# DLRM tower, one core: first two one-hot fields looked up as a couple, tile 3's rows at other places, one ScalarE copy for two lookups

## The chip, the cores and the metric

One core of one Trainium2 chip. The metric is the device time of one execution in microseconds (us); lower is better. Engines are named as in the profile: PE (TensorE matmul), PEld (its weight load), DVE (VectorE), ACT (ScalarE), POOL (GpSimd), SP (SyncE, here a DMA queue).

## What is computed

The reference, cut to what matters:

```
e  = stack([tbl_f[ids[:, f]] for f in range(26)], axis=1)   # 512 x 26 x 128, float32
T  = concatenate([r_dense[:, None, :], e], axis=1)          # 512 x 27 x 128
Z  = einsum('bnd,bmd->bnm', T, T)[:, iu0, iu1]              # 351 dot products a sample
h  = concatenate([Z, r_dense], axis=1)                      # 512 x 479
h  = maximum(h @ W_top1 + b_top1, 0)                        # 512 x 512
h  = maximum(h @ W_top2 + b_top2, 0)                        # 512 x 256
y  = h @ W_top3                                             # 512 x 1
```

Twelve of the 26 tables are large (12500 or 125000 rows) and 14 are small (1000 or 1250 rows).

## The kernel before, in words

**Small tables.** Their 14 fields (places 1 to 14 of XT) are looked up on PE. A table is cut into chunks of 128 rows: 8 chunks for the first six fields, 10 for the last eight, 128 chunks in all. A chunk's one-hot matrix `hot` (128 rows by 512 samples) is made by comparing the broadcast ids `ids_bc` with a row number, and PE multiplies the chunk with it, once for the high part `t_hi` (L473) and once for the low part `t_lo` (L475), adding up in one of six PSUM banks. ACT makes `t_hi` (L594) and DVE `t_lo` (L708). `t_hi` and `t_lo` have three places each, `table` five, `hot` eight chunks.

Fields 2 to 13 are looked up in couples: the table of an even number holds the first half of both fields' chunks, field by field in turn, the odd one the second half, so that one instruction makes the one-hots of two chunks (128x1024). Fields 0 and 1 are single (`SINGLES = 2`), each one-hot 128x512. Most one-hots are made by DVE (L739). ACT makes some in two steps: `distance` (L612, |ids - row|, into `apart`) and `one_hot` (L623, relu(1 - distance)). For the single fields that is every fifth one-hot, for tables 3 and 5 to 13 (`ACT_TABLES`) the last one of the table; table 4 has none.

A finished lookup bank is copied by ACT into XT (L636, 128x512, destination 32 floats apart), field i-2 in ACT's part of table i. PE waits for such copies only at tables 6, 8, 10 and 12, where a couple's two banks are used again. Field 12 goes by DVE (L744, L745), and field 13 by ACT (L633, L634), in two parts.

**Large tables.** POOL gathers rows by 48 indirect DMAs (L403), a tile of 128 samples and a group of four fields after the other. A step `rows (t, g)` is four PE transposes into `tp` (L457) and one copy from there into XT (L582), by ACT but for the steps in `VECTOR_ROWS`, which are DVE's: before, that is (3, 1).

**The tower.** For each of four tiles there are two halves. `burst` and `gram` are each 32 small matmuls (L431) of a half into one of two PSUM halves; ACT and DVE then drain the half, each two copies to `table` (L566) and eight to `Zt` (L574). A half's bank is used again two halves later, and `burst` waits for that drain. Some rows of Zt are moved by small DMAs (L328, L364) before layer 1 may read them. `dense` (L415, 8 matmuls) starts layer 1's sum of a tile and `layer1` (L421, 24 matmuls) ends it; DVE's relu (L773) makes h1; `layer2` is L532 and L542.

**Order.** Each engine goes through the list `timeline()` in its order: the 14 one-hot steps with the nine row steps of tiles 0 to 2 among them, then the tower's steps. PE, ACT and DVE each do their own part of a step, one after the other, and wait for semaphores. SP issues the table and id loads in the order of the tables; before, ids of table 4 wait until table 1 has been used up by PE (L337), and everything behind them in the queue waits with them.

The places of low parts in DVE's order:

```
LOW_PARTS = {(i, 5 if i < SINGLES else 4 if OH_CHUNKS[i] == 8 else 6): (i + 1, 0, OH_CHUNKS[i + 1])
             for i in range(1, K_OH - 1)}
LOW_PARTS.update({(0, 0): (0, 0, HEAD), (0, 4): (0, HEAD, OH_CHUNKS[0]), (0, 5): (1, 0, HEAD),
                  (1, 1): (1, HEAD, OH_CHUNKS[1])})
```

Of the kernel before, what the change touches and what calls it, by code (L numbers as in the profile page):

```python
# [29 lines left out]
TILES = BATCH // P  # L30
# [17 lines left out]
VECTOR_ROWS = [(3, 1)]  # L48
IDS = 6
HEADED = 2  # L50
HEAD = 3
PARTS = 3
HOTS = 8
SINGLES = 2
# [4 lines left out]
ACT_EVERY = 5  # L59
ACT_TABLES = [3, 5, 6, 7, 8, 9, 10, 11, 12, 13]  # L60
# [37 lines left out]
LOW_PARTS = {(i, 5 if i < SINGLES else 4 if OH_CHUNKS[i] == 8 else 6): (i + 1, 0, OH_CHUNKS[i + 1])  # L98
             for i in range(1, K_OH - 1)}
LOW_PARTS.update({(0, 0): (0, 0, HEAD), (0, 4): (0, HEAD, OH_CHUNKS[0]), (0, 5): (1, 0, HEAD),  # L100
                  (1, 1): (1, HEAD, OH_CHUNKS[1])})


def timeline():

    steps = []
    for i in range(K_OH):
        steps.append(("onehot", 0, i))  # L110
        steps += [("rows", t, g) for t, g in ROWS_AFTER.get(i, [])]
    steps += [("dense", 0, 0), ("burst", 0, 0), ("gram", 0, 0), ("burst", 0, 1), ("gram", 0, 1), ("rows", 3, 0),
              ("burst", 1, 0), ("gram", 1, 0), ("rows", 3, 1), ("burst", 1, 1), ("gram", 1, 1), ("burst", 2, 0),
              ("gram", 2, 0), ("layer1", 0, 0), ("layer1", 0, 1), ("burst", 2, 1), ("gram", 2, 1), ("dense", 1, 0),
# [3 lines left out]
    return steps  # L118
# [55 lines left out]
def pair_of(i):  # L174

    return i if i < SINGLES else i - (i - SINGLES) % 2


def field_of(i, c):

    return i if i < SINGLES else pair_of(i) + c % 2


def row_chunk(i, c):

# [19 lines left out]
HOT_FIRST = [k for k, i in enumerate(TABLE_OF) if i < SINGLES or (k - first_hot(i)) % 2 == 0]  # L205


def hot_width(m):

    return 1 if TABLE_OF[HOT_FIRST[m]] < SINGLES else 2  # L210


def by_scalar(m):

    i = TABLE_OF[HOT_FIRST[m]]
    if i < SINGLES:
        return m % ACT_EVERY == ACT_EVERY - 1
# [8 lines left out]
def dlrm_tower(nc, dense, ids, ids_oh, tbls, small, w1, w2, tail, ends, out):  # L226
    f32, f32r, i32 = mybir.dt.float32, mybir.dt.float32r, mybir.dt.int32
    ALU, ACT = mybir.AluOpType, mybir.ActivationFunctionType
    with ExitStack() as ctx:
# [67 lines left out]

        def lookup_bank(i):

            return work[:, (i - K_OH + GRAM_BANKS) % LOOKUP_BANKS, :]  # L300
# [31 lines left out]
        def _(sp):  # L332
            def table_ids(i):

                n = 1 if i < SINGLES else 2
                if i >= SINGLES + 2:
                    sp.wait_ge(hot_used, groups_used(first_hot(ids_free(i))))  # L337
                sp.dma_start(ids_bc[:, ids_slot(i):ids_slot(i) + n, :],
                             ids_oh[i:i + n, :, :].rearrange("f p b -> p f b")).then_inc(ids_in[i], 16)
# [246 lines left out]
        def _(act):  # L586
# [15 lines left out]
            def distance(j):  # L602
# [4 lines left out]
                act.wait_ge(ids_in[f], 16)  # L607
                act.wait_ge(rownum_ready, 2)
# [20 lines left out]
            def copy_lookups(f):  # L629
# [5 lines left out]
                else:  # L635
                    nc.scalar.copy(XT[:, :, 1 + f], lookup_bank(f)).then_inc(lookup_copied, 1)  # L636
# [5 lines left out]
            one_hot(mine_in(0)[0])  # L642
            high_part(1, 0, HEAD)
            distance(1)
            high_part(1, HEAD, OH_CHUNKS[1])
            for kind, t, i in STEPS:
                if kind == "onehot":
                    rest = mine_in(i)[1:]
                    if rest and i < HEADED:
                        one_hot(rest[0])  # L650
                    if i + 1 < SINGLES:
                        one_hot(mine_in(i + 1)[0])
                    if i + 2 < K_OH:
# [41 lines left out]
        def _(dve):  # L695
# [28 lines left out]

            low_part(*LOW_PARTS[0, 0])
            for kind, t, i in STEPS:
                if kind == "onehot":
                    f = field_of(i, 0)
                    dve.wait_ge(ids_in[f], 16)
                    n = 1 if i < SINGLES else 2  # L730
                    for c in range(0, OH_CHUNKS[i], n):
# [3 lines left out]
                        if not by_scalar(HOT_FIRST.index(k)):  # L735
                            if k >= HOTS:
                                dve.wait_ge(hot_used, groups_used(k + n - HOTS))
                            v, at = KINDS.index(OH_CHUNKS[i]), row_chunk(i, c)
                            nc.vector.tensor_scalar(hot[:, k % HOTS:k % HOTS + n, :], ids_bc[:, ids_slot(f):ids_slot(f) + n, :],  # L739
                                                    rownum[:, v, at:at + 1], None,  # L740
                                                    ALU.is_equal).then_inc(hot_dve, 1)
# [106 lines left out]
```

## Time and profile before

| what | value |
|---|---|
| times of 3 runs | 118.52, 118.72 and 598.5 us (median 118.72) |
| the profiled execution | 118.53 us, of which the span of the instructions is 116.7 us |
| granted clock of PE | 1.00 over the span |
| busy share of the span | PE 93%, PEld 78%, DVE 73%, ACT 69%, POOL 56% |
| DMA | 17.75 MB, mean 152 GB/s |

The one run of 598.5 us stands alone beside two that agree within 0.2 us. The profiled execution is 1.83 us longer than its span, which is what lies before the first and behind the last instruction. Busy shares are means over stages with different limits.

### The profile page before, as it was taken

Reading aid. Unit: us, or ns where it says so; the run is one execution under the profiler, and the core shown is the slowest. Engines: PE = TensorE matmul, PEld = TensorE weight load, DVE = VectorE, ACT = ScalarE, POOL = GpSimd, SP = SyncE. Lnnn points to the kernel's source line nnn. Section 1 sums busy time; section 2 is a strip of 40 time slices with the busy share of each in tenths; the row PEclk is TensorE's granted clock in tenths of the full one; section 3 lists DMA queues with packets and bytes.
Section 4 is the critical chain, followed back from the end, with each engine's and each line's share of the span. In section 5 each row is a group of like instructions: output and inputs, shape, how many; then the busy total and the mean of one; then the engine's idle time right before and its main releaser. Section 6 shows DMA issues by size and latency. Waiting matters only on the chain.

```text
span 116.7 us, 2626 instructions
## 1 busy us (share of the span) xinstructions
PE 108.4 (93%) x1008; PEld 91.0 (78%) x1008; DVE 85.6 (73%) x179; ACT 80.9 (69%) x151; POOL 65.3 (56%) x66
## 2 busy tenths in 40 slices
PE   4889799899999999999999999989699998998993
PEld 4757478588688887887888788978599987898990
DVE  5699999889597789969778751499996841567131
ACT  4469990994999999999997794499993602455011
POOL 7387787788777877877787775003063720004000
PEclk9999999999999999999999999999999999999999
DMA  3799749999999529992111112001011110001000
GB/s 74 262 361 406 275 105 411 382 398 363 400 316 380 218 71 367 405 338 65 45 45 32 35 45 60 13 0 26 6 23 51 34 32 6 0 3 21 6 3 1
DMA packets 7751, 17.75 MB, mean 152 GB/s; under 512 B 2078, under 2 KB 3002, under 8 KB 7610
## 3 DMA queue, kind: packets, MB, share of 16 engines
q1 hardware_dynamic: 5770, 14.13, 33.1%
q0 software_dynamic: 1824, 3.25, 9.7%
q10 hardware_dynamic: 144, 0.20, 0.6%
q8 instruction: 8, 0.13, 0.5%
q14 instruction: 5, 0.04, 0.1%
HBM read 17.33 MB, written 0.00 MB: 148 GB/s over the span
## 4 chain that ended last, share of the span: by engine, by line
PE 66%; ACT 11%; DMA 8%; DVE 8%; issue 4%; SPq 1%; ACTq 0%; DVEq 0%
PE work L473 20%; PE work L475 19%; DMA table<-small 8%; PE work L431 8%; PE work L421 6%; PE work L532 5%; ACT Zt L574 4%; PE tp L457 4%; DVE hot L739 3%; PE work L415 3%; ACT t_hi L594 2%; ACT table L566 2%; DVE Zt L574 2%; ACT hot L623 2%; DVE t_lo L708 2%
## 5 line engine op out<-in xcount | busy, mean ns | idle before, releaser
L403 POOL DMA_INDIRECT rows<-tbl,idx x48 | 58.4, 1217 | 18.3 <-issue 13.3
L473 PE MATMUL work<-hot,t_hi 128*128 128x512 f32 x128 | 51.8, 405 | 2.2 <-DVE hot L739 1.1
L475 PE MATMUL work<-hot,t_lo 128*128 128x512 f32 x128 | 50.2, 392 | 0.0
L739 DVE TENSOR_SCALAR hot<-ids_bc,rownum 128x1024 fp32r<-128x1024 int32 (+1 forms) x59 | 38.9, 699 | 7.2 <-PE work L475 7.1
L473 PEld LDWEIGHTS work<-hot,t_hi 128*128 128x128 f32 x128 | 24.0, 188 | 10.8 <-DVE hot L739 2.9
L475 PEld LDWEIGHTS work<-hot,t_lo 128*128 128x128 f32 x128 | 24.1, 188 | 4.4
L594 ACT CAST t_hi<-table 128x1280 fp32r<-128x1280 f32 (+3 forms) x16 | 16.8, 1050 | 5.8 <-DMA table<-small 5.5
L708 DVE TENSOR_TENSOR t_lo<-table,t_hi 128x1280 fp32r<-128x1280 f32 (+3 forms) x16 | 19.5, 1217 | 1.2 <-ACT t_hi L594 1.0
L431 PE MATMUL work<-XT 128*58 128x52 f32 x512 | 15.1, 217 | 2.4 <-ACT Zt L574 1.1
L431 PEld LDWEIGHTS work<-XT 128*58 128x58 f32 x512 | 14.3, 133 | 3.7 <-issue 2.4
L328 POOL DMA_DIRECT2D Zt<-table x9 | 4.7, 531 | 22.1 <-DVE table L566 22.1
L612 ACT ACTIVATE apart<-ids_bc,minus_row 128x1024 f32<-128x1024 int32 (+1 forms) x13 | 13.6, 1046 | 0.9 <-DMA ids_bc<-ids_oh 0.9
L574 DVE COPY Zt<-work 17x48 f32<-17x48 f32 (+1 forms) x64 | 12.8, 200 | 1.0
L623 ACT ACTIVATE hot<-apart 128x1024 fp32r<-128x1024 f32 (+1 forms) x13 | 12.5, 962 | 1.5 <-PE work L475 1.4
L636 ACT COPY XT<-work 128x512 f32<-128x512 f32 x12 | 13.3, 1104 | 0.0
L574 ACT COPY Zt<-work 17x48 f32<-17x48 f32 (+1 forms) x64 | 12.6, 196 | 0.8
L582 ACT COPY XT<-tp 128x512 f32<-128x512 f32 x11 | 8.2, 743 | 6.1 <-PE tp L457 5.9
L566 ACT COPY table<-work 14x224 f32<-14x224 f32 x16 | 5.7, 359 | 8.9 <-PE work L431 8.7
L566 DVE COPY table<-work 14x224 f32<-14x224 f32 x16 | 6.1, 380 | 6.2 <-PE work L431 5.9
L421 PE MATMUL work<-Zt,w_sb 128*128 128x128 f32 x84 | 10.2, 277 | 0.0
L421 PEld LDWEIGHTS work<-Zt,w_sb 128*128 128x128 f32 x84 | 9.8, 192 | 0.2
L457 PE MATMUL tp<-ident,rows 128*128 128x128 f32 x48 | 7.3, 274 | 0.0
(47 smaller groups left out, 58.1 us busy)
## 6 DMA issues: line engine op xcount, KB each, us to landing
table<-small SPq DMA_DIRECT2D x8, 640.0 KB, 7.9
ids_bc<-ids_oh SPq DMA_DIRECT2D x6, 512.0 KB, 6.1
table<-small SPq DMA_DIRECT2D x4, 512.0 KB, 7.6
w_sb<-w SPq DMA_DIRECT2D x1, 1024.0 KB, 7.7
rows<-tbl,idx POOLq DMA_INDIRECT x48, 4.1
table<-small SPq DMA_DIRECT2D x2, 320.0 KB, 5.0
ids_bc<-ids_oh SPq DMA_DIRECT2D x2, 256.0 KB, 4.5
w_sb<-w SPq DMA_DIRECT2D x1, 512.0 KB, 8.8
```

Of the source, the lines that this page charges most:

```text
L403: nc.gpsimd.indirect_dma_start(rows[:, t, place - FIRST, :], None, tbls[f], bass.IndirectOffsetOnAxis(ap=idx[:, t, place - FIRST:place - F ...
L421: last = nc.tensor.matmul(l1_block(t, u), w1_sb[:, c, u * P:(u + 1) * P], Zt[:, t, c, :], start=False, stop=c == CHUNKS - 1 and (t == TILE ...
L431: last = nc.tensor.matmul(gr[PAD * s:PAD * s + COUPLED, half, q, 0:COUPLE * FIELDS], XT[:, b:b + COUPLE, :].rearrange("d s n -> d (s n)")[ ...
L473: nc.tensor.matmul(bank, t_hi[:, i % PARTS, c * D:(c + 1) * D], hot[:, k % HOTS, :], start=row_chunk(i, c) == 0, stop=False)
L475: last = nc.tensor.matmul(bank, t_lo[:, i % PARTS, c * D:(c + 1) * D], hot[:, k % HOTS, :], start=False, stop=row_chunk(i, c) == n - 1)
L566: return copy(Zlow[:, t % 2, :, first:end:COUPLE], gr[PAD * s:PAD * s + LOW, half, :, column(s):column(s) + LOW].rearrange("n q m -> n m q"))
L574: last = copy(Zt[PAD * g:PAD * g + n, t, :, first:end:COUPLE], gr[PAD * s:PAD * s + n, half, :, column(s) + n - CHUNKS:column(s) + n].rear ...
L594: nc.scalar.copy(t_hi[:, i % PARTS, c0 * D:c1 * D], table[:, i % TABLES, c0 * D:c1 * D]).then_inc(hi_ready, 1)
L612: nc.scalar.activation(apart[:, j % 2, 0:n * BATCH].rearrange("p (f b) -> p f b", f=n), ids_bc[:, ids_slot(f):ids_slot(f) + n, :], ACT.Abs ...
L623: nc.scalar.activation(hot[:, k % HOTS:k % HOTS + n, :], apart[:, j % 2, 0:n * BATCH].rearrange("p (f b) -> p f b", f=n), ACT.Relu, bias=1 ...
L708: nc.vector.tensor_tensor(t_lo[:, i % PARTS, c0 * D:c1 * D], table[:, i % TABLES, c0 * D:c1 * D], t_hi[:, i % PARTS, c0 * D:c1 * D].bitcas ...
L739: nc.vector.tensor_scalar(hot[:, k % HOTS:k % HOTS + n, :], ids_bc[:, ids_slot(f):ids_slot(f) + n, :], rownum[:, v, at:at + 1], None, ALU. ...
```

## The change

- Fields 0 and 1 become a couple like the others (`SINGLES` is gone; all tables are interleaved). Only their first two chunks keep single one-hots (`LONE = 2`), and their ids come by two DMAs of their own at the head of SP's queue. ACT's head part of table 0 is 4 chunks and not 3; table 1 is loaded and split as a whole (`HEADED = 1`), before in two parts. The id places are counted so that the ids of table 4 wait for nothing.
- ACT makes the last one-hot of tables 0, 1, 3, 4, ... 13: table 4 is new, and tables 0 and 1 have one wide one-hot each in place of three single ones in all.
- ACT copies the two lookups of a couple by one instruction of 128x1024, in its part of the next couple's first table; fields 12 and 13 stay as they are.
- `rows (3, 0)` goes in front of the first `burst` and is copied by DVE; `rows (3, 1)` goes behind `layer1 (0, 1)` and is copied by ACT. `dense (0)` goes from in front of the first `burst` to behind `gram (0, 1)`, and `dense (2)` from behind `gram (3, 0)` to in front of `burst (3, 0)`.
- DVE's relu of tile 2 goes into the drain of the last half, in front of its last four copies.

```diff
-VECTOR_ROWS = [(3, 1)]
+VECTOR_ROWS = [(3, 0)]
-HEADED = 2
-HEAD = 3
+HEADED = 1
+HEAD = 4
-SINGLES = 2
+LONE = 2
-ACT_EVERY = 5
-ACT_TABLES = [3, 5, 6, 7, 8, 9, 10, 11, 12, 13]
+ACT_TABLES = [0, 1, 3, 4, 5, 6, 7, 8, 9, 10, 11, 12, 13]
...
+LOW_PARTS = {(i, 4 if OH_CHUNKS[i] == 8 else 6): (i + 1, 0, OH_CHUNKS[i + 1]) for i in range(K_OH - 1)}
+LOW_PARTS.update({(0, 0): (0, 0, HEAD), (0, HEAD): (0, HEAD, OH_CHUNKS[0]), (0, 6): (1, 0, OH_CHUNKS[1])})
...
-    steps += [("dense", 0, 0), ("burst", 0, 0), ("gram", 0, 0), ("burst", 0, 1), ("gram", 0, 1), ("rows", 3, 0),
-              ("burst", 1, 0), ("gram", 1, 0), ("rows", 3, 1), ("burst", 1, 1), ("gram", 1, 1), ("burst", 2, 0),
-              ("gram", 2, 0), ("layer1", 0, 0), ("layer1", 0, 1), ("burst", 2, 1), ("gram", 2, 1), ("dense", 1, 0),
-              ("layer2", 0, 0), ("layer1", 1, 0), ("layer1", 1, 1), ("rows", 3, 2), ("burst", 3, 0), ("gram", 3, 0),
-              ("dense", 2, 0), ("layer2", 1, 0), ("burst", 3, 1), ("gram", 3, 1), ("layer1", 2, 0), ("layer1", 2, 1),
+    steps += [("rows", 3, 0), ("burst", 0, 0), ("gram", 0, 0), ("burst", 0, 1), ("gram", 0, 1), ("dense", 0, 0),
+              ("burst", 1, 0), ("gram", 1, 0), ("burst", 1, 1), ("gram", 1, 1), ("burst", 2, 0), ("gram", 2, 0),
+              ("layer1", 0, 0), ("layer1", 0, 1), ("rows", 3, 1), ("burst", 2, 1), ("gram", 2, 1), ("dense", 1, 0),
+              ("layer2", 0, 0), ("layer1", 1, 0), ("layer1", 1, 1), ("rows", 3, 2), ("dense", 2, 0), ("burst", 3, 0),
+              ("gram", 3, 0), ("layer2", 1, 0), ("burst", 3, 1), ("gram", 3, 1), ("layer1", 2, 0), ("layer1", 2, 1),
...
-                if i >= SINGLES + 2:
-                    sp.wait_ge(hot_used, groups_used(first_hot(ids_free(i))))
...
+                if i >= IDS:
+                    sp.wait_ge(hot_used, groups_used(first_hot(i - IDS + 2)))
...
-            table_ids(0)
+            for f in range(LONE):
+                sp.dma_start(ids_bc[:, f, :], ids_oh[f, :, :]).then_inc(ids_in[f], 16)
...
-                    nc.scalar.copy(XT[:, :, 1 + f], lookup_bank(f)).then_inc(lookup_copied, 1)
+                    nc.scalar.copy(XT[:, :, 1 + f:3 + f],
+                                   work[:, bank_of(f):bank_of(f) + 2, :].rearrange("p f b -> p b f")).then_inc(lookup_copied, 2)
...
             high_part(0, HEAD, OH_CHUNKS[0])
-            one_hot(mine_in(0)[0])
-            high_part(1, 0, HEAD)
-            distance(1)
-            high_part(1, HEAD, OH_CHUNKS[1])
+            high_part(1, 0, OH_CHUNKS[1])
             for kind, t, i in STEPS:
                 if kind == "onehot":
...
+                    if 1 < i < K_OH - 2:
                         high_part(i + 2, 0, OH_CHUNKS[i + 2])
...
+                    for m in mine_in(i):
+                        one_hot(m)
+                        if i == 0:
+                            distance(1)
+                    if i <= 1:
+                        high_part(i + 2, 0, OH_CHUNKS[i + 2])
+                    if i > 1 and pair_of(i) == i:
                         copy_lookups(i - 2)
...
                     copy_high(nc.vector.tensor_copy, t, i, halves % HALVES, first)
+                    if t == TILES - 1 and i == 1:
+                        units_done(t - 1)
                     if t < TILES - 1 or i == 1:
                         copy_high(nc.vector.tensor_copy, t, i, halves % HALVES, second).then_inc(gram_dve, 1)
```

## Rows read from the trace of the kernel before

**Rows 1.** The page's busy times of the engines over the span.

```profile
PE 108.4 (93%) x1008; PEld 91.0 (78%) x1008; DVE 85.6 (73%) x179; ACT 80.9 (69%) x151; POOL 65.3 (56%) x66
```

**Rows 2.** PE's waits, 0 to 75 us: us in total, times, longest.

```profile
PE work L473 <- DVE hot L739: 1.1, 2, 0.7
PE work L473 <- ACT t_hi L594: 0.5, 1, 0.5
PE work L473 <- ACT hot L623: 0.4, 1, 0.4
```

**Rows 3.** The chain that ended last, at table 4: start, us, what.

```profile
24.11 0.23 PE work L475
```

**Rows 4.** Timeline, start-up: start, us, engine, line, what [idle before <-releaser].

```profile
7.50 0.49 ACT L594 CAST t_hi<-table 128x384 fp32r<-128x384 f32 x1
8.58 0.73 ACT L612 ACTIVATE apart<-ids_bc,minus_row 128x512 f32<-128x512 int32 x1 [0.58 <-DMA ids_bc<-ids_oh]
13.72 0.49 PE L473 MATMUL work<-hot,t_hi 128*128 128x512 f32 x1 [0.70 <-DVE hot L739]
```

**Rows 5.** Timeline, 15 to 31 us, tables 2 to 5.

```profile
15.83 0.47 SPq L350 DMA_DIRECT2D table<-small  x1
...
20.63 1.05 ACT L594 CAST t_hi<-table 128x1024 fp32r<-128x1024 f32 x1 [3.10 <-DMA table<-small]
...
22.68 0.50 PE L473 MATMUL work<-hot,t_hi 128*128 128x512 f32 x1 [0.42 <-ACT hot L623]
...
23.97 1.27 ACT L594 CAST t_hi<-table 128x1280 fp32r<-128x1280 f32 x1 [0.29 <-PE work L475]
...
27.99 0.74 ACT L582 COPY XT<-tp 128x512 f32<-128x512 f32 x1 [1.72 <-PE tp L457]
...
30.86 0.50 PE L473 MATMUL work<-hot,t_hi 128*128 128x512 f32 x1
```

**Rows 6.** Timeline, 72 to 84 us, the first halves of the tower.

```profile
72.76 0.94 DVE L745 COPY XT<-work 128x384 f32<-128x384 f32 x1
...
80.21 0.72 ACT L582 COPY XT<-tp 128x512 f32<-128x512 f32 x1
80.42 0.78 DVE L566 COPY table<-work 14x224 f32<-14x224 f32 x2
...
83.49 1.92 PE L431 MATMUL work<-XT 128*58 128x52 f32 x64 [1.09 <-ACT Zt L574]
```

**Rows 7.** The chain that ended last, 95 to 110 us.

```profile
95.62 0.45 PE tp L457 x4
...
96.86 1.92 PE work L431 x64
98.77 1.09 PE work L415 x8
...
106.79 0.70 DVE apart L773
...
107.54 1.99 PE work L532 x8
```

**Rows 8.** Groups by line and shape: xcount | busy us, mean ns | idle before.

```profile
L739 DVE TENSOR_SCALAR hot<-ids_bc,rownum 128x1024 fp32r<-128x1024 int32 x46 | 33.2, 757 | 7.2 <-PE work L475 7.1
L636 ACT COPY XT<-work 128x512 f32<-128x512 f32 x12 | 13.3, 1104 | 0.0
L612 ACT ACTIVATE apart<-ids_bc,minus_row 128x1024 f32<-128x1024 int32 x10 | 11.4, 1143 | 0.0
L623 ACT ACTIVATE hot<-apart 128x1024 fp32r<-128x1024 f32 x10 | 10.6, 1064 | 1.5 <-PE work L475 1.4
L594 ACT CAST t_hi<-table 128x1280 fp32r<-128x1280 f32 x8 | 10.2, 1271 | 0.3 <-PE work L475 0.3
L708 DVE TENSOR_TENSOR t_lo<-table,t_hi 128x1024 fp32r<-128x1024 f32 x4 | 4.9, 1216 | 0.0
```

**Rows 9.** Timeline of POOL: the last gather of `rows (3, 0)`.

```profile
65.77 1.02 POOL L403 DMA_INDIRECT rows<-tbl,idx  x1 [0.31 <-issue]
```

More of the change, by code:

```diff
@@ L296, in dlrm_tower, with bank_of @@
         turn_full, rows_ready, last_ready = sem("turn_full"), sem("rows_ready"), sem("last_ready")
+        def bank_of(i):
+            return (i - K_OH + GRAM_BANKS) % LOOKUP_BANKS
         def lookup_bank(i):
-            return work[:, (i - K_OH + GRAM_BANKS) % LOOKUP_BANKS, :]
+            return work[:, bank_of(i), :]
         def l1_block(t, u):
@@ L729, in _ @@
                     dve.wait_ge(ids_in[f], 16)
-                    n = 1 if i < SINGLES else 2
-                    for c in range(0, OH_CHUNKS[i], n):
+                    for c in range(OH_CHUNKS[i]):
                         if (i, c) in LOW_PARTS and i + c:
@@ L734, in _ @@
                         k = first_hot(i) + c
[L735 to L741, printed above, removed]
+                        if k not in HOT_FIRST or by_scalar(HOT_FIRST.index(k)):
+                            continue
+                        n = hot_width(HOT_FIRST.index(k))
+                        if k == 1:
+                            dve.wait_ge(ids_in[1], 16)
+                        if k >= HOTS:
+                            dve.wait_ge(hot_used, groups_used(k + n - HOTS))
+                        v, at, slot = KINDS.index(OH_CHUNKS[i]), row_chunk(i, c), ids_slot(f) + c % 2
+                        nc.vector.tensor_scalar(hot[:, k % HOTS:k % HOTS + n, :], ids_bc[:, slot:slot + n, :],
+                                                rownum[:, v, at:at + 1], None, ALU.is_equal).then_inc(hot_dve, 1)
                     if i == K_OH - 1:
@@ L768, in _ @@
                 elif kind == "layer1" and i == (1 if t < TILES - 1 else 0):
-                    if t >= 2:
+                    if t < TILES - 2:
+                        units_done(t)
+                    elif t == TILES - 1:
                         dve.wait_ge(l2_full, t - 1)
-                    if t < TILES - 1:
-                        dve.wait_ge(l1_part, 2 * (t + 1))
-                        nc.vector.tensor_scalar(h1[:, t % 2, :, :], l1[:], 0.0, None, ALU.max).then_inc(h1_ready, 1)
-                    else:
                         for u in range(0, BLOCKS, 2):
@@ L833 @@
     for i, n in enumerate(OH_CHUNKS):
-        if i < SINGLES:
-            table = chunks[i]
-        else:
-            f = pair_of(i)
-            part = slice((i - f) * n // 2, (i - f + 1) * n // 2)
-            table = np.stack([chunks[f][:, part], chunks[f + 1][:, part]], axis=2)
+        f = pair_of(i)
+        part = slice((i - f) * n // 2, (i - f + 1) * n // 2)
+        table = np.stack([chunks[f][:, part], chunks[f + 1][:, part]], axis=2)
         arrays[f"small_{i}"] = table.reshape(OH_ROWS, n * D)
```

46 lines of the change are left out of this document (16 added, 30 removed).

## The prediction, made before the changed kernel was run

> **What bounds the kernel now.** I read the page first: PE is busy 93% of the span [rows 1]. So the time is PE's work plus PE's waits, and the next views are PE's waits and the chain that ended last. Up to 75 us PE waits little: twice for a one-hot of DVE, once for a high part, once for a one-hot of ACT [rows 2]. In between it runs one matmul each 0.23 us [rows 3]: a chunk of two is 0.457 us, a table of 8 chunks 3.66 us, one of 10 chunks 4.58 us, and four transposes 0.45 us [rows 7]. That is a floor which the change doesn't touch. Only the waits can go, and they are told by the timeline of the start [rows 4], of tables 2 to 5 [rows 5], of the first halves of the tower [rows 6], and the chain near the end [rows 7]. Prices of single instructions come from the groups by shape [rows 8]. I sum against the profiled execution, 118.53 us (span 116.7 and 1.83 around it); it is 0.2 below the median of the runs shown, 118.72, which I count as no difference. What a measurement of this kernel can tell from no change is put at 2%, 2.4 us.
>
> **Part 1, start-up to the start of table 4.** Before, table 4 starts at 23.71: the matmul at 22.68 is the first of chunk 30, and two chunks lie between, 2 x 0.457 and 0.11 for the restart [rows 5]. Two waits lie ahead of it: PE stands from about 12.9 to 13.72 for chunk 13 [rows 4], and before 22.68 for ACT's one-hot, which came late because ACT had waited 3.10 us for table 5; that load was issued at 15.83 only, behind the ids of table 4, which waited for table 1 to be used up [rows 5].
> The second wait goes: ids of table 4 wait for nothing now, and table 5 is behind the low part of table 0, some 7 us earlier. Worth 0.57 and 0.11 us of restart, 0.68.
> The first is replaced by others. DVE has less to do up to the end of table 1's one-hots: 2 single ones at 0.4 and 5 wide ones at 0.67 (4.15) in place of 13 single ones (5.2), the starts in sequence being some 0.08 closer than the durations; a gain of 1.1. But ACT's chain becomes the late one. Its high part of table 1 needs the whole 512 KB of it. In the queue these end after 24 + 256 + 256 + 256 + 256 + 512 = 1560 KB (ids of the gathers, head of table 0, ids of fields 0 and 1, rest of table 0, table 1). Before, ids of field 1 ended the same 1560 KB and released ACT at 8.55 [rows 4]; the head of table 1 could be cast at 7.50 already [rows 4]. From 8.55: high part of table 1 0.95, one-hot of table 0 0.96, distance 1.04, high part of table 2 0.95 (durations of rows 8 less about 0.1 for the overlap, the 128x1024 cast taken from 1.05 in [rows 5]), that is 12.45; low part of table 2 on DVE, 1.14, then one-hot k = 12, 0.7: 14.35. PE takes chunk 12 then and ends table 1 at 14.4 + 4 x 0.457 = 16.25. Before it ended at 15.3 (13.72 + 0.11 + 3 x 0.457). So 1.0 us is lost here.
> Tables 2 and 3 then run without a wait in my count: DVE comes to k = 28 at 20.6 and has it at 21.3 while PE wants it at 21.8, and ACT has k = 30 at 22.1 against 22.7. Table 4 starts at 16.25 + 2 x 3.66 + some restart = 23.65. Sum of part 1: 1.0 lost, 0.7 and the small gaps of tables 2 and 3 won, -0.06. Bounds: it moves one to one with the landing of table 1. The earliest is 7.6 (after the 984 KB that had landed by 7.50), then -0.95, where DVE's chain also stops it; the latest I take 0.7 behind 8.55, +0.65, since ids of table 4 and table 5 now press behind it and six gathers run beside it.
>
> **Part 2, the wide copy and table 4's one-hot on ACT.** Before, ACT in table 4 is free early and stands 1.72 us before the row copy at 27.99 [rows 5], and still PE gets the last one-hot of table 5 only at 30.86, when it wanted it at 30.59: it follows the row copy and the high part of table 7 in ACT's order. The stall is 0.27 and 0.10 of restart. After: high part of table 6 from T4+0.26 (23.97 for T4 = 23.71) to T4+1.43, one-hot 0.96, distance 1.04, wide copy C less 0.1, so the row copy begins at T4+3.33+C, if that is later than T4+4.28, where the transposes end. From there 0.59, 1.15 and 1.07 to the one-hot of table 5. C is not in the trace. The nearest rows: casts with whole runs of 1280 and 384 elements take 1.27 and 0.49 us [rows 4, 5], 0.87 ns an element and 0.155 fixed. The lone copy, one element in each 128 bytes, takes 1.104 [rows 8], 1.85 ns an element; the row copy, runs of four, takes 0.74 [rows 5], 4.6 ns a run. A break thus costs some 1 ns: for runs of two, 512 x (2 x 0.87 + 1.0) + 0.155 = 1.55 us. Ends: 1.1 (breaks hidden entirely) and 2.2 (two lone copies, nothing won). I take 1.55, the row of runs of four being the nearest. Then the one-hot is there at T4+7.69 in place of T4+7.15: +0.55 us (0.15 at C = 1.1, 1.2 at C = 2.2).
> All later tables have room: an even table's ACT work is 1.17 + 0.96 + 1.04 + C + 0.6, 5.2 us at C = 1.55 against PE's 5.03, but its one-hot is taken before the copy, the next table's is wanted 3.8 us after that table starts, and an odd table's work is only 3.8. DVE gives up table 4's one-hot (0.67), which is hidden under PE and counts nothing. A copy saves ACT 0.6 us a couple, which also counts nothing while PE is the bound.
> On the wide copy the Trainium skill has a rule of its own, in "SBUF — State Buffer", section "Door 1: The DMA port swizzle (why `[64,N]` ≈ `[32,N]`)": SBUF has 16-byte lines, and an access that goes to a new line pays. By it places 1 and 2 lie in one line, but 3 and 4 in two. The rows of lone and four-element runs agree with it as well as with a price of a break. Its result is rival 2.
>
> **Part 3, the tower.** The first burst waited behind `dense (0)` and the lookup copies, and starts at 73.31. Now transposes of `rows (3, 0)` are in its place, 0.45 for 1.05, and the copies' first parts end at 72.94: start 73.0, -0.3. The gather must have landed by 72.3; its last DMA was issued at 65.77 [rows 9] and gathers take 4.1 us on the page, so 69.9. DVE's copy of it lies behind its lookup copy, which ends at 73.7 [rows 6], ends at 74.4, and the first drain begins at 75.0: free. `dense (0)` fills PE's wait for the first drain, 76.75 to 77.7: free.
> Before, ACT's copy of (3, 0) at 80.21 held up the drain, and the third tile's first burst stood 1.09 us, to 83.49 [rows 6]. Without it DVE's drain is late next: DVE's third half begins at 80.42 and takes 2.54, to 82.96. With the 0.3 earlier, burst (2, 0) starts at 82.7: -0.8 in all.
> `rows (3, 1)` was in a wait of PE and now stands in full work, before `burst (2, 1)`: +0.45. Its ACT copy meets an idle ACT.
> `dense (2)`, 1.09, goes into the wait for the copy of (3, 2). Before, from 95.62: 0.45 + 0.79 of wait + 1.92 + 1.09 = 4.24 [rows 7]. After: h1 of tile 1 is ready about 0.77 after the start (0.69 of relu and two hand-overs), then 1.09 + 1.92 = 3.78: -0.45.
> The relu of tile 2: it ended at 107.49 and layer 2 started at 107.54 [rows 7], while `dense (3)` had ended at 107.2. Now the relu is four copies (0.85) earlier, though not before layer 1's end: it ends 0.3 before dense (3) does. -0.34. The four copies behind it end 0.85 later than the relu, 1.4 before layer 1 of the last tile wants them, and the small DMAs for it are as early as all else. Sum of part 3: -0.8 + 0.45 - 0.45 - 0.34 = -1.14. Bounds: -1.5 (if rows (3, 1) hides) and -0.5 (if a small DMA of tile 0 or 3 is late, since burst (2, 0) is sooner and the DMAs' landing isn't).
>
> **Sum.** -0.06 + 0.55 - 1.14 = -0.65: 118.53 - 0.65 = 117.9 us.
>
> **Rivals.**
> 1. Start-up really gains. Table 1 lands at 7.6 to 7.9 as its own pieces did before, DVE's 1.1 us come through, and part 1 is -0.7 to -0.95: 117.0 to 117.2; with C near 1.1 as well, 116.7. For: DVE was what PE waited for twice [rows 2], and the wait at 22.68 goes for certain. Against: ACT's order puts two wide ACT steps ahead of the high part of table 2.
> 2. The copy pays for each line of 16 bytes. As a mechanism of this kernel: a lone element costs 1.85 ns, so a couple that lies in one line costs 1.1 us, one in two lines 0.155 + 512 x 2 x 1.85 ns = 2.05. The copy of fields 2 and 3 (places 3 and 4), the one in table 4, is of the second kind: part 2 is +1.05 in place of 0.55, 118.4 us. This is what the Trainium skill's rule would make of it. For: a lone element and three together give 1.85 + 3 x 0.87 = 4.5 ns, and the row copy shows 4.6. Against: a plain price of a break gives the same.
> 3. The other side: ACT becomes the bound. The wide copy reads two PSUM banks in turn, element by element, which no row shows. If each switch costs as much again as a break and C reaches 3 us, the stall of table 5 is +2.05 and an even and an odd table's ACT work is 6.7 + 3.8 = 10.5 us against PE's 10.06: +0.4 for each of three later couples. 118.53 - 0.06 + 2.05 + 1.3 - 1.14 = 120.7. It decides the sign from C = 2.2 on. Against: the row copy also reads 512 bytes apart and is cheap.
> 4. Start-up loses more: the first wide one-hots need ids of both fields, and table 1 lands at 9.2: +0.65, 118.6.
> That the change doesn't do what it says would be C = 2.2 with nothing saved; it is the end of part 2.
>
> **How the numbers follow.** Forecast (117.4 to 118.3) 0.42, rival 1 0.22, rival 2 0.16, rival 4 0.13, rival 3 0.05, the rest 0.02 for something unseen. The range leaves out rival 3 and the far ends of 1 and 4: 116.5 to 119.3. Faster by over 2% means below 116.3, which needs rival 1 at its end and part 3 at its bound: 0.11. Slower by over 2% is above 121.1, rival 3 and worse: 0.03. Within: 0.86.
>
> **What would show it.** Part 1: table 1's high part starts near 8.5, a PE wait before chunk 12, and table 4 starting near 23.65 with no wait of ACT for table 5. Part 2: a group of six copies 128x1024 with a mean near 1.55 (rival 2: three of 1.1 and three of 2.05), and a PE wait of some 0.8 in table 5 for ACT's one-hot. Part 3: the first burst near 73.5, burst (2, 0) released by DVE 9.7 us after the first, no wait longer than 0.1 before layer 2 of tile 2. The prediction is wrong if the high part of table 1 starts a microsecond from 8.5, if C is beyond 2.2, or if layer 1 of tile 0 waits for its small DMAs.

## The result, and the profile after

The changed kernel took 119.59 us (median of 12 runs, 119.25 to 120.68), the kernel before beside it 119.36; the ratio is 1.0058, with a 95% interval of 1.0031 to 1.0084. A second set of runs gave 1.0052 (1.0017 to 1.0087). So it is 0.5% slower: no change by the bound of 2%, but on the other side of where the forecast put it, and above the range. The profiled execution took 119.52 us, span 117.7, against 118.53 and 116.7. Here and below a median is of all the runs of a set, while a ratio compares only the executions in the usual one of two states that a kernel shows.

The median of the kernel before moved between 118.7 and 119.7 us from one set of runs to the next, more than most single terms here. The verdicts on terms below therefore rest on the marks of the profiles, and on the ratios only for the whole. Most marks repeat to 0.05 us; the landing of table 1 (8.04 to 9.04 us) and the stretch of tables 6 to 13 (39.5 to 41.0) don't.

The page, and PE's waits up to 75 us and behind (us in total, times, longest; they answer to [rows 1, 2]):

```profile
PE 108.7 (92%) x1008; PEld 91.6 (78%) x1008; DVE 83.5 (71%) x171; ACT 79.6 (68%) x144; POOL 62.7 (53%) x66
```

```profile
PE work L467 <- DVE hot L739: 1.4, 2, 1.3
PE work L467 <- ACT hot L619: 1.1, 1, 1.1
PE work L467 <- issue: 0.8, 1, 0.8
PE work L425 <- DVE XT L743: 0.4, 1, 0.4
...
PE work L425 <- DVE Zt L568: 1.2, 2, 0.6
PE work L409 <- DVE apart L720: 0.3, 1, 0.3
PE work L526 <- DVE apart L720: 0.3, 1, 0.3
```

DVE and ACT have less to do than before and PE waits longer for them: one wait of 1.1 us for a one-hot of ACT is new. The timeline of that place (start, us, engine, line), which answers to [rows 5]:

```profile
24.18 1.27 ACT L588 CAST t_hi<-table 128x1280 fp32r<-128x1280 f32 x1 [0.67 <-PE work L469]
25.36 1.05 ACT L619 ACTIVATE hot<-apart 128x1024 fp32r<-128x1024 f32 x1
26.32 1.14 ACT L608 ACTIVATE apart<-ids_bc,minus_row 128x1024 f32<-128x1024 int32 x1
27.36 1.99 ACT L632 COPY XT<-work 128x1024 f32<-128x1024 f32 x1
29.12 0.79 ACT L576 COPY XT<-tp 128x512 f32<-128x512 f32 x1
29.77 1.28 ACT L588 CAST t_hi<-table 128x1280 fp32r<-128x1280 f32 x1
30.93 1.08 ACT L619 ACTIVATE hot<-apart 128x1024 fp32r<-128x1024 f32 x1
...
32.05 0.50 PE L467 MATMUL work<-hot,t_hi 128*128 128x512 f32 x1 [1.10 <-ACT hot L619]
```

Read it from below: PE gets the last one-hot of table 5 at 32.05. ACT had begun it at 30.93, behind a high part, behind the row copy, which began at 29.12 although its transposes had ended at about 28.2; ahead of that stand the new one-hot of table 4, the distance for the one-hot of table 5, and a wide copy of 1.99 us.

The start-up (answers to [rows 4]):

```profile
8.66 1.05 ACT L588 CAST t_hi<-table 128x1024 fp32r<-128x1024 f32 x1 [0.67 <-DMA table<-small]
9.61 1.06 ACT L619 ACTIVATE hot<-apart 128x1024 fp32r<-128x1024 f32 x1
10.57 1.14 ACT L608 ACTIVATE apart<-ids_bc,minus_row 128x1024 f32<-128x1024 int32 x1
11.62 1.03 ACT L588 CAST t_hi<-table 128x1024 fp32r<-128x1024 f32 x1
...
12.69 1.23 DVE L698 TENSOR_TENSOR t_lo<-table,t_hi 128x1024 fp32r<-128x1024 f32 x1 [0.38 <-ACT t_hi L588]
...
14.63 0.50 PE L467 MATMUL work<-hot,t_hi 128*128 128x512 f32 x1 [0.77 <-issue]
```

This is the forecast chain, step by step: high part of table 1 as its DMA lands, one-hot, distance, high part of table 2, low part, one-hot k = 12 (of chunks 12 and 13), PE. The wait for table 5 of [rows 5] is gone.

The tower (answers to [rows 6, 7]), from the timeline:

```profile
74.57 3.62 PE L425 MATMUL work<-XT 128*58 128x52 f32 x128 [0.38 <-DVE XT L743]
...
81.73 1.92 PE L425 MATMUL work<-XT 128*58 128x52 f32 x64 [0.61 <-DVE Zt L568]
...
84.28 1.92 PE L425 MATMUL work<-XT 128*58 128x52 f32 x64 [0.62 <-DVE Zt L568]
...
88.90 0.60 PE L451 MATMUL tp<-ident,rows 128*128 128x128 f32 x4
...
97.62 1.16 PE L409 MATMUL work<-dense_t,w_sb 128*128 128x128 f32 x8 [0.35 <-DVE apart L720]
...
107.75 0.69 DVE L720 TENSOR_SCALAR apart<-work 128x512 f32<-128x512 f32 x1 [0.89 <-PE work L415]
...
108.50 1.99 PE L526 MATMUL work<-w_sb,apart 128*128 128x256 f32 x8 [0.33 <-DVE apart L720]
```

DVE's drain is late next, as forecast, with two waits of 0.6. `dense (2)` fills the wait for the copy of (3, 2). But the relu of tile 2 starts at 107.75 though its matmuls were issued by 107.0, and layer 2 still waits 0.33 us for it.

All profiles cut at the same marks, in us. `T1` is the start of ACT's high part of table 1 in the new start-up; `4` and `6` are PE's starts of tables 4 and 6; `E` is the last lookup matmul; `h0` to `h7` are the starts of the eight halves on PE:

```
kernel             T1     4      4>6   6>E    E>h0  h0>h4  h4>h5  h5>h6  h6>h7  h7>end
before             -      23.71  8.53  39.84  1.22  10.18  4.72   8.64   4.66   15.20
changed            8.66   23.93  9.51  39.93  1.20   9.71  5.16   9.28   3.77   15.19
changed, again     8.80   24.07  9.52  39.97  1.19   9.70  5.20   9.28   3.77   15.19
e1 lone copies     8.78   24.05  8.77  39.54  1.18   9.77  5.16   9.28   3.77   15.20
e2 table 4 DVE     9.04   24.31  8.58  40.96  1.19   9.69  5.16   9.36   3.77   14.85
e3 shifted XT      8.44   23.74  8.56  39.68  1.19   9.72  5.16   9.28   3.77   15.19
e4 tower alone     -      24.07  8.79  39.81  1.94   9.70  5.16   9.28   3.77   14.82
e5 waits           8.04   23.30  9.51  40.12  1.09   9.70  5.20   9.30   3.77   14.75
e6 high 2 first    8.55   23.39  9.49  39.91  1.22   9.70  5.20   9.33   3.77   15.19
e7 all three       8.78   23.62  8.56  40.25  1.08   9.70  5.16   9.28   3.77   14.75
e8 e7, rows (3,1)  8.53   23.37  8.56  39.58  1.07   9.69  4.73   9.28   3.77   14.75
e9 before, shifted -      24.43  8.45  39.62  1.22  10.03  4.92   8.52   4.66   15.18
e10 e7, lone       8.61   23.48  8.70  39.87  1.08   9.70  5.16   9.28   3.77   14.75
e11 start-up alone 8.13   23.40  8.57  39.53  1.22  10.19  4.72   8.64   4.66   15.22
```

Changed less before, first profiles: start +0.22, tables 4 and 5 +0.98, tables 6 to 13 +0.09, tower -0.31 (-0.02 - 0.47 + 0.44 + 0.64 - 0.89 - 0.01). That makes +0.98, beside +1.0 of the span and +0.99 of the profiled executions. The start's +0.22 is smaller than what the landing of table 1 alone moves it from run to run.

### The profile page after: what moved, and what is told of

Same layout as the page of the kernel before. It is cut to its first block, busy times and chain, and to the rows that moved or that the text cites. A ratio compares the mean times of both kernels' runs of the same rounds, so it can differ in the third digit from the quotient of the medians.

```text
span 117.7 us, 2615 instructions
## 1 busy us (share of the span) xinstructions
PE 108.7 (92%) x1008; PEld 91.6 (78%) x1008; DVE 83.5 (71%) x171; ACT 79.6 (68%) x144; POOL 62.7 (53%) x66
## 4 chain that ended last, share of the span: by engine, by line
PE 74%; DVE 9%; ACT 6%; DMA 4%; issue 4%; SPq 1%; ACTq 0%; DVEq 0%
PE work L467 23%; PE work L469 21%; PE work L415 8%; PE work L425 8%; PE work L526 5%; DMA table<-small 4%; DVE Zt L568 4%; PE tp L451 3%; DVE table L560 2%; PE work L409 2%; ACT hot L619 2%; PE work L536 2%; ACT t_hi L588 2%; DVE apart L720 1%; PE tp L415 1%
## 5 line engine op out<-in xcount | busy, mean ns | idle before, releaser
L397 POOL DMA_INDIRECT rows<-tbl,idx x48 | 55.8, 1163 | 20.3 <-issue 12.4
L739 DVE TENSOR_SCALAR hot<-ids_bc,rownum 128x1024 fp32r<-128x1024 int32 (+1 forms) x52 | 36.8, 742 | 8.8 <-PE work L469 6.8
L698 DVE TENSOR_TENSOR t_lo<-table,t_hi 128x1280 fp32r<-128x1280 f32 (+2 forms) x15 | 19.3, 1290 | 3.0 <-ACT t_hi L588 3.0
L588 ACT CAST t_hi<-table 128x1280 fp32r<-128x1280 f32 (+2 forms) x15 | 16.7, 1111 | 6.5 <-DMA table<-small 3.1
L322 POOL DMA_DIRECT2D Zt<-table x9 | 4.7, 531 | 23.7 <-DVE table L560 23.7
L608 ACT ACTIVATE apart<-ids_bc,minus_row 128x1024 f32<-128x1024 int32 x13 | 14.9, 1146 | 0.8 <-DMA ids_bc<-ids_oh 0.8
L619 ACT ACTIVATE hot<-apart 128x1024 fp32r<-128x1024 f32 x13 | 13.8, 1063 | 1.6 <-PE work L469 1.6
L632 ACT COPY XT<-work 128x1024 f32<-128x1024 f32 x6 | 9.3, 1551 | 0.0
```

The lines of the kernel that those rows point to most:

```text
L397: nc.gpsimd.indirect_dma_start(rows[:, t, place - FIRST, :], None, tbls[f], bass.IndirectOffsetOnAxis(ap=idx[:, t, place - FIRST:place - F ...
L588: nc.scalar.copy(t_hi[:, i % PARTS, c0 * D:c1 * D], table[:, i % TABLES, c0 * D:c1 * D]).then_inc(hi_ready, 1)
L608: nc.scalar.activation(apart[:, j % 2, 0:n * BATCH].rearrange("p (f b) -> p f b", f=n), ids_bc[:, ids_slot(f):ids_slot(f) + n, :], ACT.Abs ...
L619: nc.scalar.activation(hot[:, k % HOTS:k % HOTS + n, :], apart[:, j % 2, 0:n * BATCH].rearrange("p (f b) -> p f b", f=n), ACT.Relu, bias=1 ...
L698: nc.vector.tensor_tensor(t_lo[:, i % PARTS, c0 * D:c1 * D], table[:, i % TABLES, c0 * D:c1 * D], t_hi[:, i % PARTS, c0 * D:c1 * D].bitcas ...
```

## The experiments

**The changed kernel again** (no edit).

> The changed kernel once more, unaltered, on the chip of the three above. If the terms read from its first profile repeat: table 4 starts 0.1 to 0.4 us later than in the kernel before, from there to table 6 it takes 9.5 us (before 8.5), and from the last lookup matmul to the end 44.3. The relu of tile 2 follows its wait by 0.43 or by 0.07 us, as one or the other of the earlier profiles. Ratio to the kernel before 1.003 to 1.008.

Ratio 1.0052, 119.66 us. Table 4 started at 24.07, tables 4 and 5 took 9.52, the relu followed late again. The readings repeat. (The expectation gives 44.3 from the last lookup matmul to the end; it was 44.33.)

**e1, lone copies in the changed kernel.**

```diff
-                    nc.scalar.copy(XT[:, :, 1 + f:3 + f],
-                                   work[:, bank_of(f):bank_of(f) + 2, :].rearrange("p f b -> p b f")).then_inc(lookup_copied, 2)
+                    nc.scalar.copy(XT[:, :, 1 + f], lookup_bank(f)).then_inc(lookup_copied, 1)
...
-                    if i > 1 and pair_of(i) == i:
+                    if i > 1:
                         copy_lookups(i - 2)
```

> The changed kernel with the wide copy undone: each lookup copied by itself again, one in each table's part of ACT, everything else as changed. Theory A (the loss sits in table 5, where PE waits 1.1 us for ACT's one-hot because a two-line copy of 1.99 us was put ahead of it in table 4): a lone copy of 1.10 us stands there, the one-hot of table 5 is there 0.89 us earlier, PE's wait for ACT in table 5 falls from 1.10 to about 0.25, and the time is 0.85 below the changed kernel, a ratio to the kernel before of 0.997 to 1.000. Theory B (the time was lost in the start-up and the tower alone): the wait may shrink, but the time stays at the changed kernel's, ratio 1.005.

Ratio 0.9868 (0.982 to 0.9917), 118.60 us. By the marks tables 4 and 5 took 8.77 in place of 9.51, which is 0.74 of the expected 0.85, and tables 6 to 13 took 39.54 in place of 39.93. The ratio lies below what was expected (0.997 to 1.000) with its whole interval. Part of that is the kernel before, which ran at 119.73 in that set; e2 and e3, beside the same runs, came out as expected, so why the ratio of e1 is this low stays open. ACT's copy in table 4 and PE's wait in table 5:

```profile
27.63 1.12 ACT L632 COPY XT<-work 128x512 f32<-128x512 f32 x1
28.49 0.81 ACT L576 COPY XT<-tp 128x512 f32<-128x512 f32 x1
...
31.43 0.50 PE L467 MATMUL work<-hot,t_hi 128*128 128x512 f32 x1 [0.28 <-issue]
```

**e2, table 4's one-hot back on DVE, wide copies kept.**

```diff
-ACT_TABLES = [0, 1, 3, 4, 5, 6, 7, 8, 9, 10, 11, 12, 13]
+ACT_TABLES = [0, 1, 3, 5, 6, 7, 8, 9, 10, 11, 12, 13]
```

> The changed kernel with table 4's last one-hot back on DVE; the wide copies stay. Theory A: ACT in table 4 has 0.96 + 1.04 us less ahead of the row copy, so even the copy of 1.99 us ends before the transposes do (at table 4's start + 3.4 against + 4.2); PE's wait in table 5 goes back to about 0.2 as before, 0.9 below the changed kernel, ratio 0.997 to 1.000. Theory C (the wide copy alone is to blame, the added one-hot costs nothing): the wait in table 5 stays above 0.8 us. DVE has 0.67 us more in table 4, with no PE wait for it.

Ratio 0.999 (0.9948 to 1.0033), 119.21 us. Tables 4 and 5 took 8.58, 0.93 less, as theory A has it, though the wide copy still took 2.02. ACT stood idle again before the row copy:

```profile
25.75 2.02 ACT L632 COPY XT<-work 128x1024 f32<-128x1024 f32 x1
28.64 0.73 ACT L576 COPY XT<-tp 128x512 f32<-128x512 f32 x1 [0.87 <-PE tp L451]
```

So neither piece does it alone. Against the 8.53 of the kernel before, the one-hot of table 4 with lone copies cost 0.24 (e1), the two-line copy without that one-hot 0.05 (e2), and both together 0.98.

This run's profile has 1 us more in tables 6 to 13, with PE idle at 42.35 and 52.95, where the profile names no releaser. Both times ACT's last one-hot of the table (7 and 9) had ended 0.05 us earlier. In table 9 it stands behind a row copy that followed a wide copy of 1.97 us; the changed kernel loses 0.26 and 0.18 us at the same place in its two profiles, the restart counted in. In table 7 it stands behind a row copy that began at 39.48 though its transposes had ended at 38.17, with ACT idle for 1.28 us; why isn't shown.

**e3, XT 4 bytes later.** Couples then lie in one line of 16 bytes, and so do the groups of four.

```diff
-        XT = sb("XT", [P, BATCH, PAD])
+        XT_line = sb("XT", [P, BATCH * PAD + 4])
+        XT = XT_line[:, 1:1 + BATCH * PAD].rearrange("p (b n) -> p b n", n=PAD)
```

> The changed kernel with XT starting 4 bytes later, so that each couple of places (1 and 2, 3 and 4, ...) lies in one line of 16 bytes, and each group of four gathered places in one line too. Theory of lines: all six wide copies take 1.10 us (now three of 1.10 and three of 1.99), the row copies fall from 0.75 to 0.61 us, the wait in table 5 falls by 0.9 + 0.13, and the time is about 1.0 below the changed kernel, ratio 0.996 to 0.999. Theory of the bank switch or of where the copy stands (the odd copies are slow for another reason, for example which PSUM banks they read: fields 2, 6 and 10 read banks 4 and 5, 2 and 3, 0 and 1): the three slow copies stay at 1.99. If PE reads an XT off the 16 bytes more slowly, its small matmuls' step of 0.029 us grows and the tower gets longer.

Ratio 0.9963 (0.9926 to 1.0), 119.34 us, the profiled execution 118.09. The wide copies of the changed kernel, then those of e3 (all uses of the line: min/median/max in ns), and the row copies of e3 (mean ns; 748 in the changed kernel):

```profile
L632 ACT COPY XT<-work x6: 1099/1552/1997, 17.8 to 68.1; 128x1024 f32<-128x1024 f32 x6
```

```profile
L633 ACT COPY XT<-work x6: 1092/1106/1111, 17.6 to 66.7; 128x1024 f32<-128x1024 f32 x6
...
L577 ACT COPY XT<-tp 128x512 f32<-128x512 f32 x11 | 6.4, 586 | 9.3 <-PE tp L452 7.3 <-issue 1.9
```

Before the shift the copies of fields 0, 4 and 8 (places 1 and 2, 5 and 6, 9 and 10) took 1.10 to 1.12 us, those of fields 2, 6 and 10 (places 3 and 4, 7 and 8, 11 and 12) 1.98 to 2.00; after it all took 1.10. The banks read and the places in ACT's order are the same in both, so it is where the places lie. With XT starting on a line, lines of 16 bytes part exactly these three from the others; lines of 32 would leave places 3 and 4 fast, and lines of 8 would make all six slow. This is as a rule of the Trainium skill, "SBUF — State Buffer", section "Door 1: The DMA port swizzle (why `[64,N]` ≈ `[32,N]`)", has it, that an access which goes to a new 16-byte line pays: the trace agrees, with 1.99 against 1.10. Tables 4 and 5 took 8.56 in place of 9.51. PE's small matmuls kept their step (64 of them took 1.92 us as before, h0 to h4 9.72).

**e9, the shift in the kernel before.**

> The kernel before with only XT shifted by 4 bytes. Row copies take 0.59 us in place of 0.74, lone copies stay at 1.10, PE's stall in table 5 (0.37 with its restart) loses 0.15, and the row copy in ACT's drain loses 0.15 as well. Theory: ratio 0.996 to 0.999, so what the shift is worth in e3 is the mending of the wide copy and not a gain of its own. Rival: the shift speeds the whole kernel, ratio 0.990.

Ratio 0.9997 (0.9959 to 1.0035), 118.51 us. Tables 4 and 5 took 8.45 (-0.08), and from h0 to the end it took 43.32 (-0.09: h0 to h4 is 0.15 shorter, h4 to h5 0.20 longer, h5 to h6 0.12 shorter). So the shift by itself is worth about 0.2 us, which the ratio can't tell from nothing.

**e4, the tower's part alone**, in the kernel before: the new order of steps, `VECTOR_ROWS = [(3, 0)]` and the relu of tile 2 in the drain; nothing else of the change.

> The kernel before with the tower's part of the change alone: places of the rows of tile 3, of dense 0 and 2, the DVE copy of (3, 0) and the relu of tile 2 in the last drain. The prediction had -1.14 us for this part; the trace of the changed kernel shows -0.31 between the end of the lookups and the end of the span. If the tower's gain is the small one and stands by itself: 0.3 to 0.4 us below the kernel before, ratio 0.996 to 0.998. If the tower lost its gain only through what came before it in the changed kernel: up to 1.1 us, ratio 0.990.

Ratio 0.9884 (0.9828 to 0.994), 118.81 us, beside the same high median of before as e1. From h0 to the end it took 42.7 against 43.4 before and 43.1 changed. Mark by mark it is the changed kernel's tower (9.70, 5.16, 9.28, 3.77) but for the last, 14.82 in place of 15.19. The reason is the relu of tile 2: in this profile and that of e2 it begins 0.07 us after its wait's own instruction, in all others with that order and both waits 0.44 us. What decides between the two stays open. Ahead of h0 this profile has 0.75 us more than the others: both copies of the last lookups began that much later after PE's last matmul; why isn't shown. The marks from h0 on show -0.7, of which 0.37 is the relu's luck: that is the small gain. The ratio doesn't agree: its interval leaves out the small expectation (0.996 to 0.998) and holds the large one. As for e1, the cause of so low a ratio stays open, and the size of the tower's gain rests on the marks alone.

**e5, two edits to waits in the changed kernel.**

```diff
                     if halves == 0:
+                        pe.wait_ge(dense_copied, 1)
+                        pe.wait_ge(xt_ready, 1)
                         pe.wait_ge(lookup_copied, K_OH - 2)
                         pe.wait_ge(last_copied, 1)
                         pe.wait_ge(lookup_dve, 1)
-                        pe.wait_ge(dense_copied, 1)
-                        pe.wait_ge(xt_ready, 1)
...
-                if t >= 2:
-                    dve.wait_ge(l2_full, t - 1)
                 dve.wait_ge(l1_part, 2 * (t + 1))
```

> The changed kernel with two edits to waits only: in front of the first burst PE's waits for dense_copied and xt_ready, long fulfilled, come ahead of the three waits for the last lookup copies and not behind them; and the relu of tile 2 on DVE waits for layer 1 alone (layer 2 of tile 0, which it also waited for, is already waited for by DVE's end_tile of tiles 0 and 1). Theory: each wait that follows the late one costs PE 0.11 us, so the first burst starts 0.2 us sooner after the copies (0.35 us behind them in all other kernels); and the wait for layer 1, no longer an instruction of its own, is passed on in 0.04 us in place of 0.07 to 0.44. Time 0.2 to 0.6 us below the changed kernel. Rival: PE's start is limited by the landing of the first weights, and the 0.35 us stay.

Ratio 0.9992 (0.9957 to 1.0028), 118.93 us, 0.6% below the changed kernel's ratio in the same set. The chain that ended last at the first burst, in the changed kernel and then in e5 (start, us, what), and e5's relu:

```profile
73.80 0.42 DVE XT L743
74.22 0.35 issue
74.57 1.93 PE work L425 x64
```

```profile
73.36 0.42 DVE XT L741
73.78 0.23 issue
```

```profile
106.81 0.69 DVE L718 TENSOR_SCALAR apart<-work 128x512 f32<-128x512 f32 x1 [0.45 <-PE work L415]
```

From the copy's end to the burst it is 0.23 in place of 0.35, so 0.12 less where 0.2 was expected; and from h7 to the relu 4.83 in place of 5.27, so -0.44, which the end of the kernel gets in full (14.75 for 15.19).

**e6, ACT's start-up order.**

```diff
                     for m in mine_in(i):
                         one_hot(m)
                         if i == 0:
+                            high_part(2, 0, OH_CHUNKS[2])
                             distance(1)
-                    if i <= 1:
+                    if i == 1:
                         high_part(i + 2, 0, OH_CHUNKS[i + 2])
```

> The changed kernel with one step of ACT's start-up order turned round: the high part of table 2 comes ahead of distance(1), not behind it. Theory (PE's last wait of the start-up, before chunk 12, hangs on ACT's chain high part 1, one-hot, distance, high part 2, then DVE's low part 2 and one-hot): high part 2 ends 1.04 earlier, the low part starts behind the one-hots k = 8 and 10 at once, 0.4 to 0.5 earlier than now, PE's wait before chunk 12 falls from 0.77 to about 0.3, and table 4 starts at 23.5 in place of 23.93, all later marks with it: 0.4 below the changed kernel. Rival (DVE is the bound there, whatever ACT's order): the wait stays at 0.7 or more, and ACT's one-hot k = 14, now 0 to 1.0 later in its chain, makes a new one.

Ratio 0.9987 (0.9957 to 1.0017), 119.02 us. PE's wait before chunk 12 was 0.32, and table 4 started 14.84 us after T1; in the changed kernel, its repeat, e1, e2 and e11 it is 15.27 each time, in e5 15.26 and in e3 15.30. So the chain is ACT's, and it moves one to one with the landing of table 1.

**e11, the start-up alone** (the changed kernel with lone copies, table 4 on DVE and the tower of before).

> The start-up part alone: the changed kernel with lone copies, table 4's last one-hot on DVE and the tower as before, so against the kernel before it differs only up to table 4. Theory: table 4 starts 15.27 us after ACT's high part of table 1 does (as in three profiles of the changed kernel), that is between 23.3 and 24.1, against 23.72 and 24.07 in two profiles of the old start-up: within 0.3 us of the kernel before, ratio 0.997 to 1.003. Rival: the start-up is the part that costs, ratio above 1.004.

Ratio 1.0037 (0.9996 to 1.0079), 118.85 us, its profiled execution 117.97. Table 4 started at 23.40, T1 + 15.27. The marks say no cost; the ratio leaves up to 0.8% open.

**e7, shift, waits and order together**, and **e10**, the same with lone copies.

> The changed kernel with the shifted XT, the waits of e5 and the order of e6. If the three are independent: 1.0 + 0.4 + 0.4 us below the changed kernel, 117.7 us beside 119.5, a ratio to the kernel before of 0.984 to 0.990. If the earlier start-up only makes table 5 wait longer for ACT: 0.993.

> The kernel of e7_all_three with lone lookup copies in place of the wide ones. Theory (a wide copy saves ACT time, 1.1 us a couple, that PE never asks for): from the start of table 4 to that of table 6 it takes 8.6 to 8.8 us as in e1, all else as e7, so the time is within 0.3 us of e7. Rival: with the start-up and the row copies quicker ACT is close to the bound, and without the wide copy it is 0.5 us or more slower.

e7: ratio 0.9844 (0.9798 to 0.989), 117.44 us. e10: ratio 0.9881 (0.9836 to 0.9925), 117.53 us. e7's gains over the changed kernel are the three terms side by side: 15.27 to 14.84, 9.51 to 8.56, 1.20 to 1.08 and 15.19 to 14.75, 1.94 in all. The span of its profile is only 1.5 shorter, since table 1 landed 0.12 later and tables 6 to 13 took 0.32 more.

e10 took 0.14 more than e7 in tables 4 and 5, and 0.38 less in tables 6 to 13. There e7's profile has a stall like that of e2: PE begins the last one-hot of table 9 at 51.58, about 0.46 late, 0.06 behind ACT's one-hot, and the row copy ahead of it had begun at 48.82, with ACT idle for 1.26 us although the transposes had ended at 47.62. The medians are 117.44 and 117.53, in different sets. So the wide copy at its best price is worth 0.14 us where ACT is late, and nothing that these runs can tell for the whole.

**e8, rows (3, 1) back in a wait**: e7, with PE's four transposes of (3, 1) in front of `burst (1, 1)`, and ACT's copy of them where it was.

```diff
...
-                if kind == "rows":
+                def turn_rows(t, i):
...
+                if (kind, t, i) == ("burst", 1, 1):
+                    turn_rows(3, 1)
+                    banks += 1
+                if kind == "rows" and (t, i) != (3, 1):
+                    turn_rows(t, i)
+                    banks += 1
...
```

> The kernel of e7_all_three, with PE's four transposes of rows (3, 1) back in front of burst (1, 1), where PE waits 0.6 us for DVE's drain; ACT's copy of them stays behind its drain of (2, 0). Theory: the 0.45 us of transposes leave the path (they cost 0.43 there in the changed kernel), and every half from (2, 1) on starts 0.43 earlier: from half (2, 0) to half (2, 1) 4.7 us in place of 5.16; time 0.4 below e7. Rival: the transposes come in the way of the burst and move burst (1, 1) by as much.

Ratio 0.9862 (0.9808 to 0.9915), 117.08 us against 118.66; the profiled execution 116.63. PE's timeline:

```profile
77.23 1.92 PE L426 MATMUL work<-XT 128*58 128x52 f32 x64
79.08 0.66 PE L449 MATMUL tp<-ident,rows 128*128 128x128 f32 x4
79.75 1.92 PE L426 MATMUL work<-XT 128*58 128x52 f32 x64
...
84.14 2.94 PE L416 MATMUL work<-Zt,w_sb 128*128 128x128 f32 x24
87.02 1.92 PE L426 MATMUL work<-XT 128*58 128x52 f32 x64
```

The transposes fill what was a wait of 0.61 before the burst at 79.75, and h4 to h5 is 4.73 in place of 5.16. It is the shortest version tried, 1.6 us below the kernel before and 0.45 below e10 by the medians of one set of runs. Even so it is 1.4% by its ratio, inside the bound of 2%, and the ratio doesn't part it from e7's 0.9844.

## Why the prediction was wrong

**The forecast** was -0.65 us; the marks give +0.98, the ratios +0.7 and +0.6. It had the stages, the chain of the start-up and the place of the new wait in table 5 right. The 1.63 us between -0.65 and +0.98 are 0.83 of part 3, 0.43 of part 2, 0.28 of part 1, and 0.09 in tables 6 to 13. The error of part 3 is the largest and alone turns the sign.

**Part 1, right in mechanism, 0.28 off.** Forecast 23.65, measured 23.93. Table 1 landed 0.11 later than 8.55, and the chain behind it was 15.27 us and not 15.10. The wait for table 5 went, and a lost microsecond took its place, as forecast. Over all profiles the old start-up reaches table 4 at 23.7 to 24.4 and the new one (e6's order aside) at 23.3 to 24.3. So the forecast -0.06 lies within this spread, and that the first pair of profiles differs by +0.22 shows no loss.

**Part 2, the price of the wide copy, mis-sized by 0.43.** The forecast took C = 1.55 us for every wide copy, from a price of a break, and +0.55; the step that failed is the choice of the row copy's reading as a break and not as lines. The six copies do average 1.55, but as three of 1.10 and three of 1.99, and the one that counts is a slow one. Rival 2 had worked this out from the same rows: 2.05 for the copy and +1.05, which puts the one-hot of table 5 at table 4's start + 8.2 (7.15 + 1.05). Measured: 1.99 and 8.12, and +0.98 for tables 4 and 5. e3 shows that lines are the cause, e1 and e2 that the loss needs the copy and the one-hot of table 4 together. The sentence that the other tables have room nearly held: tables 6 to 13 took 0.09 more, with a small new wait for ACT's one-hot in table 9, behind the two-line copy of table 8.

**Part 3, forecast -1.14, measured -0.31, the largest error.** The drain: -0.5 of the forecast -0.8 came (h0 to h4 -0.47), with DVE late next as said. Rows (3, 1): +0.44 for +0.45. What failed:

- "The copies' first parts end at 72.94: start 73.0, -0.3." This prices the hand-over from the copies to the burst at 0.06, and it took 0.35: PE has further waits to go through, each an instruction of its own. With `dense (0)` gone, E to h0 stayed at 1.2. Before, `dense (0)` had only filled the same time without a gap, from the last lookup to 0.37 behind the copies' first parts (two rows below). e5 took 0.12 of the hand-over away by order alone.
- "Now the relu is four copies (0.85) earlier, though not before layer 1's end: it ends 0.3 before dense (3) does. -0.34." It moved ahead of the copies, but began 0.44 us after its wait's instruction, a hand-over that the drain's copies had covered before. h7 to the end was unchanged. Without the second wait, e5, e7, e8 and e10 got 0.44.
- `dense (2)`: -0.25 (h5 to h7) for -0.45. h5 to h6 grew by 0.64, as worked out (0.77 + 1.09 for 0.45 + 0.79, +0.62), but h6 to h7 fell by 0.89 and not by the 1.09 of `dense`: before, it had added only 1.00 there from its first matmul to layer 2's, and layer 2 of tile 1 takes 1.92 to the next burst in place of 1.82.

The end of `dense (0)` and the first burst before (start, us, engine, line; no idle time between):

```profile
72.33 1.05 PE L415 MATMUL work<-dense_t,w_sb 128*128 128x128 f32 x8
73.31 3.62 PE L431 MATMUL work<-XT 128*58 128x52 f32 x128
```

**Rivals.** 2 was the one, and with part 3 as measured it gives 118.53 - 0.06 + 1.05 - 0.31 = 119.2. Neither 1 (table 1 landing at 7.6 to 7.9) nor 4 (at 9.2) occurred in any profile: the landings lie at 8.04 to 9.04, and the start of table 4 moved with them one to one, as worked out. 3 did not occur: the switch of banks cost nothing that shows, since the copies in one line take as long as a lone one of half the size.

## What to carry to other kernels

When a strided copy's price is guessed, look at where its elements lie in memory and not only at how long its runs are: the average was right and the one copy on the path cost 0.44 us more. Before an engine gets more work in the slack of one stage, add up everything that stands in its order ahead of the next thing another engine waits for; here two additions cost 0.24 and 0.05 us by themselves, and 0.98 together. And a gain counted as "starts as soon as X is ready" needs the hand-over priced: put waits long fulfilled ahead of the late one, and drop a wait that another one already implies.

## What the runs showed of the hardware

- A ScalarE copy from PSUM of 128x1024 floats into pairs 128 bytes apart took 1.10 us where both floats of a pair lie in 16 aligned bytes, and 1.99 us where they don't; a lone float each 128 bytes took 1.10 us for 512. Runs of four took 0.586 us in one line and 0.748 in two. The DVE copy of a group of four took 0.69 to 0.72 us in the five profiles with the shift and 0.71 to 0.87 in the nine without, so for DVE a difference isn't shown.
- A chain of waits on one engine costs after the last one is fulfilled. On PE, 0.36 to 0.39 us lay between the end of the late copies and the first burst where further waits followed the late one (the seven profiles in which PE stood idle there), and 0.25 with two of them moved ahead (e5, e7, e8, e10). On DVE it was 0.04, from layer 1's last matmul to the relu, where the relu waited for one thing only (the same four).
- The same two-wait relu began 0.07 us or 0.44 us after its wait's instruction, 0.44 in five profiles (the changed kernel twice, e1, e3, e6) and 0.07 in two (e2, e4). Not settled.
